# A graph network kernel: one-hots of the bucket count laid out by pairs of chunks, and last blocks zeroed in 19 calls of 128 lanes

## The chip, the cores and the metric

The kernel runs on one NeuronCore of a Trainium2 chip, the other seven idle. Its time is the device time of one execution in microseconds. A core has four compute engines, which are programmed separately and meet only at semaphores: PE (TensorE, matrix products into PSUM), DVE (VectorE), ACT (ScalarE) and POOL (GpSimd). SP (SyncE) only issues DMAs. POOL issues the indirect DMAs, whose row numbers come from a table in SBUF, one row per lane (partition).

## The reference

6250 nodes of 128 features, 100000 edges (source, target, a vector of 128, a type, a weight) sorted by target. Four graph layers follow each other, each with a sum over edges, dense products, and a normalisation:

```python
edge_index = jnp.stack([src, dst])
x = _layernorm(x + L0(x, edge_attr_128, ..., edge_index, batch0))    # edge vectors summed by source, MLP with batch norms
x = _layernorm(x + L1(x, edge_index, W, b))                          # mean of x[src] by target
x = _layernorm(x + L2(x, edge_index, edge_type_3, Wmsg, ...))        # mean of typed messages by target
x = _layernorm(x + L3(x, edge_index, edge_weight, W, ...))           # weighted, degree-normalised sum by target
```

Sums over edges are `segment_sum(rows[src], dst)`, or in L0 `segment_sum(edge_attr, src)`. The change touches none of the layers. It touches only how the kernel sorts its edges before the first one.

## The kernel before, in words

The nodes lie in 49 groups of 128 (`GROUPS`). Each edge belongs to one of 49 x 49 = 2401 buckets, by the group of its source and the group of its target. The kernel first writes all edges into a DRAM array `slots`, bucket after bucket, each bucket rounded up to blocks of four rows (`BLK`). With edges sorted so, a tile of 128 rows touches one group of nodes, and sums and gathers become products with one-hot matrices. This sorting comes in stages:

1. *Lists and keys* (to 11.5 us). SP loads sources, targets, types and weights as 128 x 784 tables. DVE shifts them to group numbers, `sg[:, 0, :]` (64 times the source's group) and `sg[:, 1, :]` (the target's), as bf16. POOL makes constants, `group_e` among them: `group_e[p, k, g, c]` is g, or 64 g for the source side, the same for all 14 values of c.
2. *Bucket count*. The 784 columns are handled in 56 batches of 14 (`HB`). `hot_pairs` (L1459) makes the one-hots of a batch for sources and targets in one DVE operation, `hot1[:, s]`, in two buffers s. `count_buckets` (L1085) makes seven matmuls of 98 x 98 (`PAIR`): each takes two chunks of 128 edges at once, chunks j and j + 7, and adds up the counts in PSUM. PE waits for `hot1_ready`, DVE for `hot1_used` of the batch before the last. After the last batch DVE copies the 98 x 98 table, of which only the parts where both chunks are the same are used.
3. *Tables* (85 to 92 us). DVE and PE turn the counts into first blocks (`first_b`), in a chain of small operations. `last_b` holds each bucket's last block, or a number out of range where the bucket is empty. It has 49 x 50 entries: one column is filled with a number out of range (L1502), so that 2450 = 98 x 25.
4. *Zeroing*. The last block of a bucket may be partly empty, so all its four rows (2176 B) are written with zeros first. SP sends `last_b` to DRAM (L483), waits, and reads it back as 98 x 25 (L485). POOL waits for both (`last_out`), makes 25 indirect DMAs of 98 lanes (L626), and waits until all have landed (L629).
5. *Scatter* (130 to 1500 us). 112 batches of seven chunks (`CB`), in a ring of four (`ARING`). For each: DVE makes one-hots (`show`), PE counts and looks up start rows (`count_batch`, `look_up`), ACT copies counts (L769) and edge payloads (L772), DVE works out row numbers (`place`, L1566), POOL scatters seven chunks (L642), SP refills edge rows and keys once the ring's buffer is free.

The order of SP's queue is written out by hand: lists, zero blocks of the spare region, edge rows, keys, node features, weights, then the index table (L482 to L485), then keys and edges of the ring. POOL's: constants, payload tables (L614 to L619, up to 29 us), waits (L621 to L624), zeroing, scatter. DVE starts the scatter batches without waiting for the zeroing; only POOL stands behind it. After 1500 us come the layers.

## Time and profile before

| | |
|---|---|
| median of 3 runs | 4760.21 us (4743.07 to 4760.88) |
| the profiled execution | 4730.64 us, span 4728.8 us |
| PE / DVE / ACT / POOL busy | 3121.7 / 2448.9 / 1101.7 / 1891.8 us |
| bucket count | 11.5 to 85 us |
| tables, index table out and back | 85 to 95 us |
| zeroing with its landing | 95 to 130.6 us |
| scatter | 130.6 to 1500 us |
| the four layers | 1500 to 4729 us |

The span is from the first to the last instruction on the core; all positions in time below count from its start. In the groups, the busy time of an engine is the time in which it executes, and "idle before" is how long it stood still ahead of these instructions, with what ended most of that. "SPq" or "POOLq" is the engine's queue, which issues DMAs. A DMA's duration on such a row is that of its issue, not of its transfer. Durations of a PE matmul overlap those of its neighbours.

### The profile page before, as it was taken

What the parts mean: (1) busy time and instruction counts of PE and PEld (TensorE: products, weight loads), DVE (VectorE), ACT (ScalarE), POOL (GpSimd) and SP (SyncE); (2) the same over time, 40 slices, a digit from 0 to 9 for tenths busy, and PEclk for the clock granted to TensorE, in tenths of its full rate; (3) what the DMA queues carried; (4) which work ended last, traced back from release to release, by engine and by line L of the source; (5) the groups of instructions that cost most, each with busy time, mean ns of one, the idle gap of its engine ahead of it and who ended that gap; (6) DMA issues with size and microseconds to landing.
All of it is one profiled execution on the core that took longest, in us unless ns stands there. A gap on an engine that the chain in (4) does not pass through costs nothing. (4 is left out here: it accounts for less than half of the span.)

```text
span 4728.8 us, 90919 instructions
## 1 busy us (share of the span) xinstructions
PE 3121.7 (66%) x22101; PEld 2714.0 (57%) x22102; DVE 2448.9 (52%) x6634; ACT 1101.7 (23%) x3584; POOL 1891.8 (40%) x1876
## 2 busy tenths in 40 slices
PE   7233333333334888677688788888888985777896
PEld 6121212122213775567678668888887875676785
DVE  6344445445445778422277743333335775222687
ACT  0010100000000114444322222111113206666302
POOL 3545456555553002466500035555554303556000
PEclk9999999999999999788899898888999997888998
DMA  6333333333333772566577344333336753666784
GB/s 193 107 95 101 95 107 107 111 108 105 107 112 105 237 235 81 172 220 222 176 237 231 121 139 127 122 120 121 127 104 196 230 176 122 210 217 208 221 265 141
DMA packets 499448, 736.58 MB, mean 156 GB/s; under 512 B 79317, under 2 KB 308702, under 8 KB 498382
## 3 DMA queue, kind: packets, MB, share of 16 engines
q1 hardware_dynamic: 404958, 498.38, 35.5%
q0 software_dynamic: 94448, 237.72, 13.7%
q8 instruction: 17, 0.28, 0.0%
q14 instruction: 25, 0.20, 0.0%
HBM read 486.89 MB, written 294.76 MB: 165 GB/s over the span
## 5 line engine op out<-in xcount | busy, mean ns | idle before, releaser
L688 POOL DMA_INDIRECT gbuf<-ring_raw,idx_blk x731 | 731.1, 1000 | 1167.2 <-DMA msg_rows<-big 425.1
L1206 PE MATMUL ps<-ring_raw,hot_raw 128*128 128x128 f32 (+2 forms) x8256 | 1027.4, 281 | 163.1 <-DVE hot_raw L1617 108.0
L1206 PEld LDWEIGHTS ps<-ring_raw,hot_raw 128*128 128x128 f32 x8256 | 969.9, 193 | 232.4 <-DVE hot_raw L1617 103.1
L642 POOL DMA_INDIRECT slots<-ring_raw,idx_edges x782 | 765.7, 979 | 607.2 <-DVE ring_raw L1566 362.4
L1232 PE MATMUL ps<-big,hot_raw 128*128 x5160 | 661.1, 293 | 124.1 <-ACT ring_raw L841 67.1
L1232 PEld LDWEIGHTS ps<-big,hot_raw 128*128 128x128 f32 x5160 | 643.8, 208 | 141.9 <-issue 140.9
L1130 PE MATMUL ps<-big 49*128 49x98 f16 x784 | 159.8, 256 | 564.8 <-ACT big L769 417.3
L1130 PEld LDWEIGHTS ps<-big 49*128 49x128 f16 x784 | 103.5, 136 | 589.8 <-issue 589.8
L1635 DVE TENSOR_TENSOR big<-big,ps 128x128 f32 (+2 forms) x1032 | 294.5, 285 | 255.1 <-PE ps L1206 216.1
L1617 DVE SCALAR_TENSOR_TENSOR hot_raw<-ring_raw,back,lane_ids 128x512 f32<-128x512 f32 x516 | 386.0, 748 | 64.0 <-DMA ring_raw<-gbuf 33.6
L1121 PE MATMUL ps<-big 128*49 128x343 bf16 (+6 forms) x784 | 264.2, 490 | 228.5 <-DVE big L1520 143.0
L1243 PE MATMUL ps<-big,hot_raw 128*128 x2064 | 315.2, 315 | 130.9 <-issue 76.5
L1243 PE MATMUL ps<-X,hot_raw 128*128 x2064 | 313.4, 313 | 121.2 <-issue 85.1
L841 ACT COPY ring_raw<-ps 128x512 f32<-128x512 f32 x473 | 277.0, 589 | 486.3 <-PE ps L1232 311.0
L1243 PEld LDWEIGHTS ps<-big,hot_raw 128*128 128x128 f32 x2064 | 291.5, 224 | 153.3 <-issue 150.8
L1243 PEld LDWEIGHTS ps<-X,hot_raw 128*128 128x128 f32 x2064 | 292.0, 225 | 142.9 <-issue 142.0
L1539 DVE TENSOR_TENSOR big<-big 49x49 f32<-49x49 f32 x112 | 22.9, 204 | 665.4 <-ACT big L769 517.4
L1663 DVE TENSOR_SCALAR hot_raw<-zr,row_t 128x512 f32<-128x512 bf16 x387 | 165.6, 487 | 322.0 <-PE ps L1232 158.6
L1121 PEld LDWEIGHTS ps<-big 128*49 128x49 bf16 x784 | 113.8, 159 | 372.8 <-issue 226.0
L1625 DVE TENSOR_TENSOR hot_raw<-dst_lane,lane_ids 128x1024 f32<-128x1024 f32 x258 | 318.2, 1234 | 14.2 <-issue 14.2
L769 ACT CAST big<-ps 49x343 f16<-49x343 f32 x112 | 49.3, 440 | 1142.3 <-remote 729.8
L1672 DVE TENSOR_SCALAR hot_raw<-zr,row_t 128x512 f32<-128x512 bf16 x258 | 126.2, 505 | 356.6 <-remote 147.8
(262 smaller groups left out, 3760.3 us busy)
## 6 DMA issues: line engine op xcount, KB each, us to landing
ring_raw<-gbuf SPq DMA_DIRECT2D x774, 268.0 KB
ring_raw<-slots SPq DMA_DIRECT2D x258, 272.0 KB
ring_raw<-in_edge_attr SPq DMA_DIRECT2D x111, 448.0 KB
zr<-lane_rows SPq DMA_DIRECT2D x387, 128.0 KB
zt<-lane_rows SPq DMA_DIRECT2D x344, 128.0 KB
pays_raw<-key_rows SPq DMA_DIRECT2D x112, 224.0 KB
big<-src_rows SPq DMA_DIRECT2D x112, 112.0 KB
slots<-ring_raw,idx_edges POOLq DMA_INDIRECT x782
```

What stands on the lines that cost most here:

```text
L642: pool.indirect_dma_start(edges, bass.IndirectOffsetOnAxis(idx_edges[0:n, u, j:j + 1], 0), edge_rows[0:n, u, j, :], None).then_inc(scatter ...
L688: pool.indirect_dma_start(gbuf, bass.IndirectOffsetOnAxis(idx_blk[:, r:r + 1], 0), node_rows[:, r, :], None, bounds_check=NBLK - 1, oob_is ...
L841: ins = act.copy(rows[:, :, 0:D], parts)
L1121: ins = pe.matmul(counts_of(s)[:, j * GROUPS:].rearrange("p (n g) -> p n g", g=GROUPS), hot2[:, s, 0, :, j], hot2[:, s, 1, :, j][:, None, ...
L1130: pe.matmul(to, hot, bases[:, s, 0, :], start=True, stop=False, skip_group_check=True)
L1206: ins = pe.matmul(bank(r % 3, width), hots[:, r, j * P:(j + 1) * P], rows[:, j, 0:width], start=j == 0, stop=j == BLK - 1)
L1232: ins = pe.matmul(bank(r)[:, j * P:(j + 1) * P], hots3[:, (odd + r) % 2, t, j * P:(j + 1) * P], msgs_flat[:, bass.ds(at[r] + t * D, D)], s ...
L1243: ins = pe.matmul(bank(r)[:, j * P:(j + 1) * P], hots[:, r, j * P:(j + 1) * P], nodes[:, bass.ds(at[r], D)], start=True, stop=True)
L1617: dve.scalar_tensor_tensor(out=hots[:, r, :].rearrange("p (k d) -> p k d", k=BLK), in0=key.broadcast_to([P, BLK, P]), scalar=back[:, k, ba ...
L1625: dve.tensor_tensor(hot_raw[:, 2 * h * BLK * P:(2 * h + 2) * BLK * P].rearrange("p (k d) -> p k d", d=P), lane.broadcast_to([P, 2 * BLK, P ...
L1635: dve.tensor_tensor(to, to, bank(r % 3, width), ALU.add).then_inc(added, 1)
L1663: ins = dve.tensor_scalar(hots3[:, (odd + r) % 2, t, :], lane_bc[r // LANE_SETS][:, r % LANE_SETS, :], row_t[:, t:t + 1], None, ALU.is_equal)
```

## The change

The one-hots get another layout. Before, `hot1[p, s, k, g, c]` had the 14 chunks innermost, and chunks j and j + 7 formed a pair: an operand of a matmul was every seventh element. Now `hot1[p, s, k, j, g, c]` has seven pairs j outside, and the two chunks of a pair (2j and 2j + 1) innermost, so an operand is 98 elements in a row. The comparison has four dimensions in this layout, so it is made in two operations of 686 elements, sources and targets apart. Which chunks form a pair doesn't change the counts.

The index table loses its extra column: 2401 entries are 18 x 128 + 97. It is read back by two DMAs, 128 x 18 and 97 x 1, and POOL makes 18 calls of 128 lanes and one of 97. POOL waits for `last_out` at 48, not 32.

```diff
--- before.py
+++ after.py
@@ -95,9 +95,9 @@
 ROW_G = D + 6
 AW = D + 5
 NOWHERE = 1.0e6
-LASTB = 25
-LASTP = 98
-assert LASTB * LASTP == GROUPS * (GROUPS + 1)
+LASTB = GROUPS * GROUPS // P
+LASTP = GROUPS * GROUPS - LASTB * P
+assert 0 < LASTP <= P
 
 HALF = STEP * P // 2
 EPS = 1e-5
@@ -172,7 +172,7 @@
         msg_rows = dram("msg_rows", [GROUPS * P * TYPES, D])
         key_rows = dram("key_rows", [COLS, P], I16)
         src_rows = dram("src_rows", [COLS, P], BF16)
-        last_blocks = dram("last_blocks", [GROUPS, GROUPS + 1], U32)
+        last_blocks = dram("last_blocks", [GROUPS, GROUPS], U32)
 
         X = sb("X", [P, GROUPS, D])
         big = sb("big", [P, 2 * GROUPS * D + GROUPS * AW])
@@ -206,7 +206,7 @@
             assert at + n <= GROUPS * AW
             return sums_flat[:, at:at + n], at + n
         hot1_f, at = work(0, 2 * GROUPS * HB)
-        hot1 = hot1_f.bitcast(BF16).rearrange("p (s k g c) -> p s k g c", s=2, k=2, g=GROUPS)
+        hot1 = hot1_f.bitcast(BF16).rearrange("p (s k j g c) -> p s k j g c", s=2, k=2, g=GROUPS, c=2)
         hot2_f, at = work(0, 2 * GROUPS * CB)
         hot2 = hot2_f.bitcast(BF16).rearrange("p (s k g c) -> p s k g c", s=2, k=2, g=GROUPS)
         src_hot_f, at = work(2 * GROUPS * HB, CB * P)
@@ -269,8 +269,8 @@
         first_b = sb("first_b", [GROUPS, 2, GROUPS])
         heads = sb("heads", [GROUPS, 12])
         heads_i = sb("heads_i", [GROUPS, 2], I32)
-        last_b = sb("last_b", [GROUPS, GROUPS + 1], U32)
-        zero_idx = sb("zero_idx", [LASTP, LASTB], U32)
+        last_b = sb("last_b", [GROUPS, GROUPS], U32)
+        zero_idx = sb("zero_idx", [P, LASTB + 1], U32)
         key_bc = pays_raw[:, COLS * PAY:COLS * PAY + ARING * CB * P // 2].bitcast(I16).rearrange(
             "p (s n) -> p s n", s=ARING)
         rank = sb("rank", [P, 2, CB])
@@ -482,8 +482,10 @@
             sp.wait_ge(last_ready, 1)
             sp.dma_start(last_blocks, last_b[:, :]).then_inc(last_out, 16)
             sp.wait_ge(last_out, 16)
-            sp.dma_start(zero_idx[:, :], last_blocks.rearrange("a b -> (a b)").rearrange(
-                "(p k) -> p k", k=LASTB)).then_inc(last_out, 16)
+            flat = last_blocks.rearrange("a b -> (a b)")
+            sp.dma_start(zero_idx[:, 0:LASTB], flat[0:P * LASTB].rearrange("(p k) -> p k", k=LASTB)).then_inc(last_out, 16)
+            sp.dma_start(zero_idx[0:LASTP, LASTB:LASTB + 1], flat[P * LASTB:GROUPS * GROUPS].rearrange(
+                "(p k) -> p k", k=1)).then_inc(last_out, 16)
 
             def next_keys(r, a):
                 if not first_of(r):
@@ -620,13 +622,14 @@
 
             pool.wait_ge(zero_done, 16 * 2 * ZSPAN // (P * BLK))
             pool.sem_inc(issued, 1)
-            pool.wait_ge(last_out, 32)
+            pool.wait_ge(last_out, 48)
             pool.sem_inc(issued, 1)
-            for k in range(LASTB):
+            for k in range(LASTB + 1):
+                n = P if k < LASTB else LASTP
                 pool.indirect_dma_start(
-                    slots, bass.IndirectOffsetOnAxis(zero_idx[:, k:k + 1], 0), zeros[0:LASTP, 0:BLK * ROW_A], None,
+                    slots, bass.IndirectOffsetOnAxis(zero_idx[0:n, k:k + 1], 0), zeros[0:n, 0:BLK * ROW_A], None,
                     bounds_check=NBLK - 1, oob_is_err=False).then_inc(last_zero, 16)
-            pool.wait_ge(last_zero, 16 * LASTB)
+            pool.wait_ge(last_zero, 16 * (LASTB + 1))
             pool.sem_inc(issued, 1)
 
             edges = slots.rearrange("b (k w) -> (b k) w", k=BLK)
@@ -1084,9 +1087,9 @@
 
             def count_buckets(b, s):
                 pe.wait_ge(hot1_ready, b + 1)
-                left, right = (hot1[:, s, k].rearrange("p g c -> p (g c)") for k in range(2))
+                left, right = (hot1[:, s, k].rearrange("p j g c -> p j (g c)") for k in range(2))
                 for j in range(HB // 2):
-                    ins = pe.matmul(ps[0:PAIR, 0, 0:PAIR], left[:, j::HB // 2], right[:, j::HB // 2],
+                    ins = pe.matmul(ps[0:PAIR, 0, 0:PAIR], left[:, j, :], right[:, j, :],
                                     start=first_of(b) and j == 0, stop=True, skip_group_check=True)
                 ins.then_inc(hot1_used, 1)
 
@@ -1457,8 +1460,11 @@
             dve.wait_ge(consts, 12)
 
             def hot_pairs(b, s):
-                dve.tensor_tensor(hot1[:, s], sg[:, :, None, bass.ds(b * HB, HB)].broadcast_to([P, 2, GROUPS, HB]),
-                                  group_e[:, :, :, :], ALU.is_equal).then_inc(hot1_ready, 1)
+                for k in range(2):
+                    ins = dve.tensor_tensor(hot1[:, s, k], sg[:, k, bass.ds(b * HB, HB)].rearrange(
+                        "p (j c) -> p j c", c=2)[:, :, None, :].broadcast_to([P, HB // 2, GROUPS, 2]),
+                                            group_e[:, k, None, :, 0:2].broadcast_to([P, HB // 2, GROUPS, 2]), ALU.is_equal)
+                ins.then_inc(hot1_ready, 1)
 
             for s in range(2):
                 hot_pairs(s, s)
@@ -1499,10 +1505,9 @@
             link(dve.tensor_scalar(next_rows, first_b[:, 0, :], float(BLK), -float(CENTRE), ALU.mult, ALU.add))
             link(dve.tensor_copy(bases[:, 0, 0, 0:GROUPS], next_rows))
             mark(dve.tensor_tensor(bases[:, 0, 1, 0:GROUPS], next_rows, bases[:, 0, 0, 0:GROUPS], ALU.subtract))
-            mark(dve.tensor_scalar(last_b[:, GROUPS:GROUPS + 1], heads[:, 0:1], 0.0, NOWHERE, ALU.mult, ALU.add))
             link(dve.tensor_scalar(blocks_f[:, 2, :], blocks_f[:, 0, :], 0.0, NOWHERE, ALU.is_equal, ALU.mult))
             link(dve.tensor_tensor(blocks_f[:, 2, :], blocks_f[:, 2, :], blocks_f[:, 0, :], ALU.add))
-            link(dve.scalar_tensor_tensor(out=last_b[:, 0:GROUPS], in0=first_b[:, 0, :], scalar=-1.0,
+            link(dve.scalar_tensor_tensor(out=last_b[:, :], in0=first_b[:, 0, :], scalar=-1.0,
                                           in1=blocks_f[:, 2, :], op0=ALU.add, op1=ALU.add))
             dve.sem_inc(last_ready, 1)
             dve.wait_ge(tables_turned, 4)
```

## Rows read from the trace of the kernel before

**Rows 1.** Table of stretches: length, each engine's busy us, granted clock, DMA share, GB/s.

```profile
95.00:128.00 33.00, 12.12 (x84) 7.42 (x82) 16.30 (x69) 1.72 (x6) 25.26 (x25) 1.00 0.62 193
130.00:1500.00 1370.00, 454.60 (x3007) 277.49 (x3008) 656.60 (x2615) 87.83 (x325) 765.05 (x782) 1.00 0.33 102
```

**Rows 2.** Waits, POOL, 130 to 1500 us: waiter, releaser, total us, times, longest.

```profile
POOL slots L642 <- DVE ring_raw L1566: 362.4, 50, 10.6
```

**Rows 3.** Timeline, 126 to 160 us: start, length, instruction, idle before and releaser.

```profile
130.57 0.99 POOL L642 DMA_INDIRECT slots<-ring_raw,idx_edges  x1 [2.82 <-issue]
...
147.01 0.96 POOL L642 DMA_INDIRECT slots<-ring_raw,idx_edges  x1 [0.30 <-issue]
...
149.86 0.44 ACT L769 CAST big<-ps 49x343 f16<-49x343 f32 x1 [40.38 <-remote]
...
154.54 1.01 POOL L642 DMA_INDIRECT slots<-ring_raw,idx_edges  x1 [6.57 <-DVE ring_raw L1566]
```

**Rows 4.** One-hots: 30 to 82 us (busy us, mean ns, idle); all (ns, first, last start).

```profile
L1460 DVE TENSOR_TENSOR big<-big,group_e 128x1372 bf16<-128x1372 bf16 x43 | 37.6, 874 | 16.3 <-PE ps L1089 16.3
...
L1460 DVE TENSOR_TENSOR big<-big,group_e x56: 859/874/1828, 11.5 to 82.6; 128x1372 bf16<-128x1372 bf16 x56
```

**Rows 5.** Timeline, 28 to 33 us: weight loads and one-hots of the bucket count.

```profile
30.21 2.29 PEld L1089 LDWEIGHTS ps<-big 128*98 128x98 bf16 x14 [0.20 <-DVE big L1460]
30.40 0.87 DVE L1460 TENSOR_TENSOR big<-big,group_e 128x1372 bf16<-128x1372 bf16 x1 [0.24 <-PE ps L1089]
...
32.89 0.87 DVE L1460 TENSOR_TENSOR big<-big,group_e 128x1372 bf16<-128x1372 bf16 x1 [0.24 <-PE ps L1089]
```

**Rows 6.** Timeline, 84 to 99 us: the index table out and back, first zeroing call.

```profile
90.44 0.14 DVE L1502 TENSOR_SCALAR last_b<-heads 49x1 uint32<-49x1 f32 x1
...
91.23 0.27 SPq L483 DMA_DIRECT2D last_blocks<-last_b  x1
...
92.54 0.32 SPq L485 DMA_DIRECT2D zero_idx<-last_blocks  x1
92.90 0.38 SPq L460 DMA_DIRECT2D pays_raw<-key_rows  x1
...
95.19 1.20 POOL L626 DMA_INDIRECT slots<-hot_raw,zero_idx  x1 [66.11 <-issue]
```

**Rows 7.** By line (L626, L688: ns min/median/max, first, last start; L439: landing us).

```profile
L626 POOL DMA_INDIRECT slots<-hot_raw,zero_idx x25: 956/961/1758, 95.2 to 126.8; - x25
...
L688 POOL DMA_INDIRECT gbuf<-ring_raw,idx_blk x731: 966/974/1406, 1921.5 to 4388.4; - x183
...
DMA to landing us min/median/max: 2.6/4.0/4.2
```

**Rows 8.** Timeline, 11.5 to 24 us: transposes and one-hots beside POOL.

```profile
11.56 1.54 PEld L1097 LDWEIGHTS ps<-ident_h,big 128*112 128x112 bf16 x14 [11.24 <-issue]
...
21.56 3.25 DVE L1460 TENSOR_TENSOR big<-big,group_e 128x1372 bf16<-128x1372 bf16 x2 [0.83 <-PE ps L1089]
```

**Rows 9.** DVE groups by form, 130 to 1500 us.

```profile
L1550 DVE TENSOR_TENSOR big<-ps,big 128x686 f32<-128x686 f32 x110 | 133.6, 1214 | 17.3 <-remote 17.3
L1555 DVE TENSOR_REDUCE found<-big 128x14 f32<-128x686 f32 x110 | 95.4, 868 | 3.8
L1520 DVE TENSOR_TENSOR big<-big,group_e 128x686 bf16<-128x686 bf16 x108 | 61.3, 568 | 11.0 <-issue 10.9
```

**Rows 10.** DVE groups by form, whole span: strided statistics reads.

```profile
L1703 DVE TENSOR_TENSOR mv<-stats 128x49 f32<-128x49 f32 x3 | 0.7, 246 | 0.1
L1703 DVE TENSOR_TENSOR mv<-stats 128x14 f32<-128x14 f32 x4 | 0.7, 184 | 0.1
```

**Rows 11.** Timeline, 90.9 to 136 us: two DVE operations in a row.

```profile
96.62 0.55 DVE L1520 TENSOR_TENSOR big<-big,group_e 128x686 bf16<-128x686 bf16 x1
...
97.09 0.44 DVE L1523 TENSOR_SCALAR big<-big,row 49x896 f16<-49x896 bf16 x1
```

## The prediction

> **What bounds the kernel now.** I read the table of time stretches first. From 130 to 1500 us the kernel scatters the edges: PE is 33%, DVE 48%, POOL 56% busy, DMA share 0.33; nothing is saturated [rows 1]. The list of POOL's waits says who holds whom there: 362 us of POOL's idle time ends with the DVE line that finishes a batch's positions [rows 2]. The timeline of that stage's start shows the reverse link: POOL's calls for the second batch end at 147.97 us (147.01 + 0.96), ScalarE's copy of the fourth batch's counts comes at 149.86, 40 us after its last instruction, and POOL's third batch follows at 154.54 [rows 3]. So the stage is a loop through POOL's own calls and their landing, and it is anchored at POOL's first scatter call. I expect a shift of that call (130.57 us) to reach the end of the kernel unchanged; what is left to ask is how far the change moves it.
>
> Two stretches lie ahead of that call. The first counts buckets in 56 batches: a DVE one-hot operation, then seven PE matmuls. The DVE operations start between 11.5 and 82.6 us; those after 30 us take 874 ns each, a row of 1372 bf16, and DVE is idle for 16.3 us waiting for PE [rows 4]. The timeline shows the rhythm: DVE starts at 30.40 and 32.89, two batches in 2.49 us, and PE's weight loads run 14 in 2.29 us without a gap [rows 5]. One batch costs 1.245 us, of which PE has 1.15. The second stretch zeroes the last blocks: the index table goes out (91.23), comes back (92.54), POOL makes 25 calls from 95.2 to 126.8, and the scatter starts 2.8 us after the last one ends [rows 3, 6, 7].
>
> **Fewer zeroing calls.** A POOL call takes 0.96 us with 0.30 idle ahead, 1.26 [rows 3]. 25 calls become 19 (18 of 128 lanes, one of 97), so 6 x 1.26 = 7.6 us go, if 128 lanes cost POOL what 98 do. They do in a near row: a 128-lane scatter of rows of almost the same length takes 974 ns in the median against 961 here [rows 7]; 19 x 0.013 = 0.2 us at most. The same 2401 rows of 2176 B (5.2 MB) now go out in 25 us, not 33, beside the other traffic: 193 GB/s at a DMA share of 0.62 [rows 1] becomes some 240 GB/s at 0.77. That is no saturation, so the wait for the last landing stays; for the lost slack I allow 1 us in the range.
>
> **A second read of the index table.** The tail of 97 indices is one more SP issue, and POOL waits for three landings in place of two. SP issues such transfers 0.36 us apart (92.54, 92.90) [rows 6], the lower bound. The old loads of 32 lanes x 4 B took up to 4.2 us to land [rows 7]; the table's way out was over after 1.3 us (91.23 to 92.54), so 4.2 - 1.3 + 0.4 = 3.3 us is the upper bound. I take 1.3 us, nearer the lower end, because the tail goes into an empty queue and is 97 elements long. Queued behind it on SP is the key load of the fourth batch; its keys are used long before POOL's third batch can go, so the delay is hidden. Behind POOL's wait stands only the zeroing.
>
> The Trainium skill ("DMA: Bandwidth & Descriptors", why a DMA increments its semaphore by 16) says that a transfer is spread over the largest number of DMA engines up to 16 that divides its slowest dimension; 97 is prime, so the tail would run on one. No row of before has such a transfer. By this rule the tail lies in the upper half of the bounds, at 2 us and not 1.3, and the sum is 0.7 us smaller.
>
> **The removed fill of the table's extra column** takes half of its 0.14 us from the DVE chain ahead of the table's way out, since DVE's instructions overlap by about that [rows 6]: 0.1 us.
>
> **The counting matmuls.** Both operands were read at a step of 14 bytes; now they are contiguous. A matmul with its load costs 164 ns now (2.29 us for 14). The nearest contiguous row is the 14 transposes of 112 x 128 bf16 at 11.56 us: 14 weight loads in 1.54 us, 110 ns each [rows 8]; seven cost 0.75 us at most. PE stops being the slower of the pair.
>
> **The one-hots.** One operation of 1372 elements becomes two of 686, whose table operand is now read two elements (4 bytes) at a time, 28 bytes apart; the key operand repeats one 4-byte word 49 times. What such a read costs is the step on which the sum turns.
> - 686 f32 contiguous take 868 ns [rows 9]: 1.04 ns each over a fixed 152 ns. The operation now, 874 = 152 + 686 x 1.05, moves two elements per tick.
> - Lower bound, short rows cost nothing: 152 + 343 x 1.04 = 509 ns.
> - Rows of seven bf16, the nearest by form: 568 ns for 686 elements [rows 9]. Pairs still run; the excess is 59 ns over 98 rows.
> - One source that hops at every element: 686 take 1214 ns [rows 9], 1.55 ns per tick.
> - Both sources hop by 24 bytes: 14 elements 184 ns, 49 elements 246 ns [rows 10], 1.77 ns per tick. Upper bound with pairs: 152 + 343 x 1.77 = 759 ns.
> I take 1.55, since one source hops and every tick does: 684 ns. Two operations in a row start 0.08 us closer than their length (0.55 long, the next 0.47 later, 96.62 and 97.09) [rows 11], so DVE's pace is 2 x 0.60 = 1.20 us per batch. The other limit, one buffer's cycle, is now 1.15 for PE + 0.87 for DVE + 0.47 of hand-over = 2.49; it becomes 0.75 + 0.60 + 0.68 + 0.40 = 2.43, or 1.21 per batch. From 30 to 82.6 us 42 x (1.245 - 1.21) = 1.5 us are gained. PE's gain is real, and DVE eats it.
>
> Before 30.4 us POOL works beside DVE, and six of the DVE operations last 1.2 to 1.8 us, as the two in 3.25 us at 21.56 [rows 8]; the excess is 3.5 us in all, in part hidden by DVE's waiting. With DVE the limit it is exposed: 13 x 1.21 + 3.5 = 19.2 us against 18.9 now (11.5 to 30.4), 0.3 lost. After the last batch PE has 0.4 us less to do. With the removed fill the counting stage gains 1.5 - 0.3 + 0.4 + 0.1 = 1.7 us.
>
> The Trainium skill ("Vector Engine (DVE) Microarchitecture Reference", 5.2, measured stream behaviour) speaks against this part: a port keeps its full rate only with runs of at least two adjacent 4-byte words, and one source that hops every word costs 1.73 ns per column. By that figure a batch costs DVE 1.33 us, the counting stage loses some 5 us, and the whole change gains 1. The rows show the effect at 1.55; none shows it with packed pairs.
>
> **Sum.** -7.6 + 1.3 - 1.7 = -8.0 us. The profiled execution took 4730.6 us (span 4728.8), so 4722.6 on its scale. It lies 29.6 us under the median of the runs shown, 4760.2, and 12.4 under the lowest; on the median's scale the forecast is 4752.
>
> **The rivals.**
> *B. Short rows are free.* The rows of seven speak for it (their 59 ns could be pairs that straddle rows, and with rows of two none does); the 1214 ns row speaks against. DVE 2 x 0.43; the cycle 0.75 + 0.43 + 0.51 + 0.40 = 2.09, 1.05 per batch: 42 x 0.195 = 8.2, before 30.4 us 3.5, with the rest 12.2. Sum -7.6 + 1.3 - 12.2 = -18.5: 4742. With PE at 80 ns per matmul it is 0.97 per batch and -23: 4737.
> *C. The repeated word counts as a hop too.* 759 - 83 = 676 ns, 1.35 per batch: +4.4, before 30.4 us +2.2, -0.5, and the zeroing's -6.3 is used up: 4760. For it speaks the 1.77; against it that only one source moves between words.
> *D. Rows of two lose the pair mode (slower than before).* The change then doesn't do what it says: DVE takes 686 ticks at 1.04 to 1.55 ns, 0.78 to 1.13 us per operation, 1.57 to 2.26 per batch. 42 batches lose 14 to 43 us, the 13 before 30.4 us 5 to 14; less 6.3 and 0.5, +12 to +50: 4772 to 4810. It is slower than before from 0.68 us per operation on. The rows of seven kept the mode, which speaks against.
> *E. The earlier start is not passed on:* the scatter loop meets its keys or edge rows later, and the time stays at 4760. Against it stands the link from landing to call above.
>
> **How the numbers follow.** Forecast 0.48, B 0.27, C 0.09, D 0.07, E 0.09. The runs before spread over 18 us, which adds to every case. 4728 to 4774 takes in B, C, E and the near end of D, and leaves out 0.1 on either side. About 0.5% (24 us) is what a measurement can tell from no change: faster than 4736 takes B's far end or a lucky spread, 0.12; slower than 4784 takes D, 0.06; the same 0.82.
>
> **What would show it.** One-hot operations of about 0.68 us, 1.21 us per batch and DVE hardly idle after 30 us; 0.51 and 1.05 mean B, 0.76 C, over 0.85 D. Weight loads 110 ns apart or less, and PE waiting for DVE. 19 zeroing calls 1.26 us apart, the first 4.0 us after the first read-back's issue, not 2.65. The first scatter call near 122.6 us, and the end of the scatter stage as much earlier. The prediction is wrong if that call moves by over 15 us or later, or if the stage behind it keeps its old end.

## Result: 0.3% slower, and the profile after

The changed kernel takes 4765.85 us in the median of 20 runs, the kernel before 4752.60 of 20 beside it: ratio 1.0032, 95% interval 1.0017 to 1.0047, so some 13 us slower where I forecast 8 us faster. The profiled execution of after took 4762.6 us with a span of 4760.7.

The timeline of POOL in the kernel after, from the payload operations to the first scatter calls (start, length, operation, idle before it):

```profile
10.31 1.93 POOL L616 MEMSET pays_raw<- 128x784 f32 x1
12.12 83.22 POOL L618 TENSOR_SCALAR pays_raw<-big 128x784 f32<-128x784 int32 x3
95.20 1.58 POOL L619 COPY pays_raw<-big 128x784 f32<-128x784 f32 x1
96.65 2.92 POOL L620 TENSOR_SCALAR pays_raw<-big 128x784 f32<-128x784 int32 x1
99.46 2.91 POOL L621 TENSOR_SCALAR pays_raw<-big 128x784 f32<-128x784 int32 x1
106.05 1.22 POOL L629 DMA_INDIRECT slots<-hot_raw,zero_idx  x1 [3.68 <-issue]
...
128.29 0.98 POOL L629 DMA_INDIRECT slots<-hot_raw,zero_idx  x1 [0.30 <-issue]
129.57 2.18 POOL L629 DMA_INDIRECT slots<-hot_raw,zero_idx  x1 [0.30 <-issue]
144.32 0.99 POOL L645 DMA_INDIRECT slots<-ring_raw,idx_edges  x1 [12.57 <-DVE ring_raw L1571]
```

The first scatter call, the anchor of the prediction, comes at 144.32 us; it was 130.57 [rows 3]: 13.75 us later. That is about what the median lost, though the interval alone would allow 8 to 22 us. The two profiled executions themselves lie 32 us apart (4762.6 and 4730.6): besides the 13.75 us, the scatter stage lasts 1387.0 us from its first call to its last in the one and 1369.2 in the other, though no line of that stage was changed.

Three things are to be seen in the rows. The first zeroing call comes 10.9 us later than 95.19 [rows 3, 6]. The 19 calls are as quick as forecast, one per 1.28 us, and end at 131.75, 25.7 us after the first one starts; before it was 32.56 (95.19 to 127.75). But behind the last one, which alone lasts 2.18 us, POOL stands idle for 12.57 us in place of 2.82 [rows 3]. The releaser named there, DVE's L1571, is a line of the stage's positions: it had written the first batch's at 114.94 us already, so the wait was for a DMA, the zeroing's own landing, as the experiments below show.

The ledger of the move is 10.86 + (25.70 - 32.56) + (12.57 - 2.82) = 10.86 - 6.86 + 9.75 = 13.75 us.

Where the first 10.86 come from, the count stage of after shows. DVE's group of instructions from 30 to 82 us (count, busy us, mean ns, idle before):

```profile
L1464 DVE TENSOR_TENSOR big<-big,group_e 128x686 bf16<-128x686 bf16 x77 | 52.7, 755 | 0.0
```

PE's group in the same stretch:

```profile
L1092 PE MATMUL ps<-big 128*98 128x98 bf16 x270 | 31.6, 288 | 20.8 <-DVE big L1464 20.8
```

The one-hot line over the whole kernel (lengths in ns min/median/max, first and last start):

```profile
L1464 DVE TENSOR_TENSOR big<-big,group_e x112: 746/756/1417, 11.9 to 89.0; 128x686 bf16<-128x686 bf16 x112
```

The table of time stretches (PE, PEld, DVE, ACT and POOL busy, granted clock, DMA share, GB/s):

```profile
30.00:50.00 20.00, 11.95 (x104) 9.53 (x102) 20.00 (x30) 0.00 (x0) 20.00 (x1) 1.00 0.93 252
50.00:70.00 20.00, 12.16 (x105) 9.86 (x105) 20.00 (x31) 0.00 (x0) 20.00 (x1) 1.00 0.69 176
```

A one-hot takes 756 ns, not 684. DVE has no idle time at all (16.3 us of it before [rows 4]), PE waits for it for 20.8 us, and POOL is "busy" from end to end with one single operation, its second payload comparison (same list of groups, 30 to 82 us):

```profile
L618 POOL TENSOR_SCALAR pays_raw<-big 128x784 f32<-128x784 int32 x1 | 77.1, 77106 | 0.0
```

The other comparisons of that size take about 3 us. A batch takes 1.37 us (weight loads at 28.32, 29.68 and 31.05 below), against 1.245 [rows 5]. PE did become quick: seven weight loads run in 0.66 us, 94 ns each, at the same granted clock of 1.00. The timeline of after, 28 to 33 us:

```profile
28.32 0.66 PEld L1092 LDWEIGHTS ps<-big 128*98 128x98 bf16 x7 [0.72 <-DVE big L1464]
29.68 0.66 PEld L1092 LDWEIGHTS ps<-big 128*98 128x98 bf16 x7 [0.70 <-DVE big L1464]
31.05 0.66 PEld L1092 LDWEIGHTS ps<-big 128*98 128x98 bf16 x7 [0.72 <-DVE big L1464]
```

So the copy of the 98 x 98 table comes at 90.67 us; in before it is at 85.00. That is 5.7 us. Then comes DVE's chain of small operations up to the index table (timeline of after):

```profile
90.67 0.26 DVE L1478 COPY tables<-ps 98x98 f32<-98x98 f32 x1 [0.91 <-PE ps L1092]
91.82 0.77 DVE L1484 CAST small_i<-tables 49x49 int32<-49x49 f32 x1
92.63 0.67 DVE L1485 TENSOR_SCALAR small_i<-small_i 49x49 int32<-49x49 int32 x1
...
94.44 2.36 DVE L1495 COPY heads<-tables 49x2 f32<-49x2 f32 x1
...
100.94 0.20 DVE L1510 SCALAR_TENSOR_TENSOR last_b<-first_b,tables 49x49 uint32<-49x49 f32 x1
```

The same chain in the kernel before (timeline, 84.5 to 96 us):

```profile
85.00 0.26 DVE L1472 COPY tables<-ps 98x98 f32<-98x98 f32 x1 [1.48 <-PE ps L1089]
...
87.70 0.16 DVE L1489 COPY heads<-tables 49x2 f32<-49x2 f32 x1
...
90.94 0.20 DVE L1505 SCALAR_TENSOR_TENSOR last_b<-first_b,tables 49x49 uint32<-49x49 f32 x1
```

10.3 us in after, 5.9 in before. A copy of 49 x 2 numbers lasts 2.36 us, and 0.16 us in before. POOL's payload operations, which before had ended by 29.1 us, run just here: the one that was held for 77 us ends at about 92.4, soon after DVE's first idle time (0.91 us ahead of the copy at 90.67), and the rest follows until 102.37. That makes 4.3 us. The last 0.9 is the second read-back: 4.91 us from the end of L1510 to the first zeroing call in after, 4.05 in before.

### The profile page after: what moved, and what is told of

Its sections match the earlier page's. It is cut to its first block, busy times and chain, and to the rows that moved or that the text cites. A ratio compares the mean times of both kernels' runs of the same rounds, so it can differ in the third digit from the quotient of the medians.

```text
span 4760.7 us, 91017 instructions
## 1 busy us (share of the span) xinstructions
PE 3107.1 (65%) x22101; PEld 2692.3 (57%) x22102; DVE 2478.0 (52%) x6689; ACT 1101.7 (23%) x3584; POOL 1963.0 (41%) x1870
## 4 chain that ended last, share of the span: by engine, by line
PE 31%; another core or an unknown queue 22%; issue 18%; DVE 11%; DMA 6%; ACT 5%; DVEq 3%; SPq 2%; POOL 1%; ACTq 1%; POOLq 0%
PE ps L1235 11%; PE ps L1209 10%; PE ps L1246 3%; DMA gbuf<-ring_raw,idx_blk 2%; PE ps L1124 2%; DMA ring_raw<-slots 2%; ACT ring_raw L841 2%; DMA ring_raw<-gbuf 2%; DVE hot_raw L1630 2%; DVEq L428 1%; DVE hot_raw L1622 1%; POOL gbuf L691 1%; PE ps L1283 1%; DVE big L1464 1%
## 5 line engine op out<-in xcount | busy, mean ns | idle before, releaser
L1668 DVE TENSOR_SCALAR hot_raw<-zr,row_t 128x512 f32<-128x512 bf16 x387 | 164.9, 488 | 321.1 <-PE ps L1235 147.4
L841 ACT ACTIVATE ring_raw<-ps,pays_raw 128x128 f32<-128x128 f32 x1032 | 280.3, 412 | 27.0 <-remote 12.7
```

Of the source, the lines that this page charges most:

```text
L841: ins = act.activation(rows[:, j, 0:D], parts[:, j, :], ACT.Copy, scale=pays_raw[:, bass.ds(at * (BLK * PAY) + (j * PAY + P_W), 1)])
```

## The experiments

The kernels are called by their first letters, a to k, where that is plain.

All ratios are against runs of the kernel before on the same chip at the same time. Beside the kernels a to d the kernel before took 4160 us in the median, beside e to g 4165, and beside h to k 4747. Most of that difference is in the scatter stage (998 to 999 us from its first call to its last there, 1360 to 1387 in the other traces), the rest behind it. One chip showed both, so it is no matter of the chip; its cause wasn't looked for. POOL's scatter calls show what it means for this document. The group of these calls in the kernel before and in `c_after_pad` (below), whole span:

```profile
L642 POOL DMA_INDIRECT slots<-ring_raw,idx_edges x782 | 765.7, 979 | 607.2 <-DVE ring_raw L1566 362.4 <-issue 244.8
L646 POOL DMA_INDIRECT slots<-ring_raw,idx_edges x782 | 761.1, 973 | 241.2 <-issue 238.1 <-DVE ring_raw L1573 3.0
```

In the second, as in all seven traces a to g, POOL goes from call to call with 0.30 us between (241 to 254 us idle for 782 calls), so the stage is as long as its calls, wherever it starts. In the other six traces POOL stands idle for 598 to 635 us, 359 to 410 of them for DVE's positions, and there the stage's length varies. The stages up to the first scatter call agree: the copy of the 98 x 98 table comes at 84.97 to 85.40 us in the five traces with the old one-hots and the early payload operations (before, b, d, f, h). By these stages I read the experiments.

**The two halves apart, and the last call with 128 lanes.** My theory was the ledger above: the late landing comes from the last call's 97 lanes, and the first call's delay from the one-hots.

`a_hots_only`: the new layout (`hot1`, `hot_pairs`, `count_buckets`), zeroing as before.

```
-                dve.tensor_tensor(hot1[:, s], sg[:, :, None, bass.ds(b * HB, HB)].broadcast_to([P, 2, GROUPS, HB]),
-                                  group_e[:, :, :, :], ALU.is_equal).then_inc(hot1_ready, 1)
+                for k in range(2):
+                    ins = dve.tensor_tensor(hot1[:, s, k], sg[:, k, bass.ds(b * HB, HB)].rearrange(
+                        "p (j c) -> p j c", c=2)[:, :, None, :].broadcast_to([P, HB // 2, GROUPS, 2]),
+                                            group_e[:, k, None, :, 0:2].broadcast_to([P, HB // 2, GROUPS, 2]), ALU.is_equal)
+                ins.then_inc(hot1_ready, 1)
```

> The kernel before with the new one-hot layout alone; zeroing stays at 25 calls of 98 lanes. Theory (ledger of the two traces: the one-hots cost 5.7 us themselves, and the payload operations of GpSimd that they push behind the count stretch VectorE's table chain by another 4.3): first zeroing call at 105.2 us, first scatter call at 140.6 (130.6 + 10.0), no late landing (under 3 us from the last zeroing call's end to the first scatter call), time +10 us against before (ratio 1.0021). Rival 1 (late landing comes from the shifted start, which meets other traffic, and not from the last call's 97 lanes): the first scatter call comes over 8 us after the last zeroing call here too. Rival 2 (start is not passed on, the scatter stage's rhythm made the 13 us): the time stays within 3 us of before although the first scatter call is 10 us later.

Measured: first zeroing call 105.29, first scatter call 140.66 us, 2.86 us idle ahead of it; 1.0026 (1.0016 to 1.0037), +11 us.

`b_zero_only`: the zeroing of after, one-hots as before.

```
-LASTB = 25
-LASTP = 98
+LASTB = GROUPS * GROUPS // P
+LASTP = GROUPS * GROUPS - LASTB * P
```

> The kernel before with the zeroing in 19 calls alone (18 of 128 lanes, the last of 97); one-hots as before. Theory (the last call's 97 rows all go out by one DMA engine): first zeroing call 96.1 us (+0.9 for the second read-back), last call's end 121.8, then some 12.5 us until the first scatter call at 134.4, +3.8 us against before; time +4 us (1.0008). Rival 1: the landing wait stays under 3 us, first scatter call at 124.6, time -6 us. Rival 2: the time doesn't follow the first scatter call.

Measured: 1.0015 (1.0004 to 1.0025), +6 us. The timeline of POOL at the end of the zeroing:

```profile
119.53 0.97 POOL L629 DMA_INDIRECT slots<-hot_raw,zero_idx  x1 [0.30 <-issue]
120.81 2.18 POOL L629 DMA_INDIRECT slots<-hot_raw,zero_idx  x1 [0.30 <-issue]
135.99 0.98 POOL L645 DMA_INDIRECT slots<-ring_raw,idx_edges  x1 [13.00 <-issue]
```

The late landing stands here with the old one-hots. The half that I had priced at -6.3 us makes the kernel slower by itself.

`c_after_pad` and `d_zero_pad`: the last call has 128 lanes, in the kernel after and in `b_zero_only`.

```
+            dve.memset(zero_idx[:, LASTB:LASTB + 1], 1000000).then_inc(padded, 1)
...
-                n = P if k < LASTB else LASTP
...
-                    slots, bass.IndirectOffsetOnAxis(zero_idx[0:n, k:k + 1], 0), zeros[0:n, 0:BLK * ROW_A], None,
+                    slots, bass.IndirectOffsetOnAxis(zero_idx[:, k:k + 1], 0), zeros[:, 0:BLK * ROW_A], None,
```

> The kernel after, but the last zeroing call has 128 lanes, too: the 31 lanes beyond the table hold 1000000 and are skipped by the bounds check. The read-back of 97 indices is unchanged. Theory (one DMA engine for 97 lanes): wait from the last call's end to the first scatter call 2.8 us in place of 12.6, first scatter call at 134.6, time 9.8 us under after's, +4 against before (1.0008). Rival 1 (fuller calls queue up in the DMA engines, or the traffic beside it is late): the wait stays over 8 us, time as after's (1.003).

> The kernel before with the zeroing in 19 calls of 128 lanes (31 of the last padded and skipped), one-hots as before. Theory: both costs are gone, first zeroing call 96.1, first scatter call at 124.6 (130.6 - 6.0), time -6 us against before (0.9987). Rival 1: late landing stays, +4 us. Rival 2 (start not passed on): 0.

Measured: c first scatter call 134.87 us, 1.0020 (1.0010 to 1.0030), +8 us; d 124.44 us, 0.9994 (0.9982 to 1.0006), -2.5 us. The same stretch of `d_zero_pad`:

```profile
119.15 0.97 POOL L630 DMA_INDIRECT slots<-hot_raw,zero_idx  x1 [0.30 <-issue]
120.43 0.97 POOL L630 DMA_INDIRECT slots<-hot_raw,zero_idx  x1 [0.30 <-issue]
124.44 0.96 POOL L646 DMA_INDIRECT slots<-ring_raw,idx_edges  x1 [3.03 <-DVE ring_raw L1570]
```

31 lanes more, and the last call takes 0.97 us and not 2.18, the wait 3.03 and not 13.00. Traffic, fuller calls and the shifted start are the same as in b, so that rival falls. In all four the scatter stage lasts 998 to 999 us from the first call to the last (c: 134.9 to 1133.3; d: 124.4 to 1122.0), so the start is passed on to that stage's end in full. In the total it can't be shown so finely: c lies 4 us above and d 3.5 above what the start says, which is the edge of c's interval and within d's.

Why 97 lanes land late, the transfers of after show, taken as a table of time stretches (DMA share and GB/s are the last two columns):

```profile
100.00:128.00 28.00, 10.07 (x61) 5.85 (x61) 14.77 (x69) 1.14 (x4) 19.43 (x18) 1.00 0.60 210
134.00:142.60 8.60, 5.44 (x47) 3.78 (x47) 7.63 (x29) 0.57 (x2) 0.00 (x0) 1.00 0.07 23
142.60:145.00 2.40, 0.57 (x2) 0.24 (x3) 2.30 (x9) 0.00 (x0) 0.68 (x1) 1.00 0.00 0
```

The packets of 134 to 142.6 us in the view of the DMA:

```profile
DMA packets 45, 0.20 MB, mean 23 GB/s; under 512 B 1, under 2 KB 1, under 8 KB 44
```

From 134 to 142.6 us a share of 0.07, about one DMA engine of sixteen (0.0625), moves 0.20 MB, of which 0.18 are 44 packets of POOL's queue; the 97 rows of 2176 B are 0.21 MB. The Trainium skill ("DMA: Bandwidth & Descriptors", why a DMA increments its semaphore by 16) has the rule that I applied to the read-back of the tail alone; this scatter's share of one engine agrees with it: 97 is prime, 98 is 14 x 7, 128 is 16 x 8.

One thing more stands in the counts of the DMA's packets, and it belongs to the cost. POOL's queue (packets, MB, share of 16 engines) over the whole zeroing, in the kernel before (25 calls of 98 lanes, 95 to 129.5 us) and in `f_all97` below (25 calls of 97 lanes, 96 to 204 us); then all packets of after from 130.5 to 134 us, just ahead of the 44 above:

```profile
q0 software_dynamic: 2000, 5.23, 48.2%
...
q0 software_dynamic: 20000, 5.37, 33.0%
...
DMA packets 776, 0.05 MB, mean 14 GB/s; under 512 B 766, under 2 KB 766, under 8 KB 776
```

A call of 98 lanes leaves as 80 packets, one of 97 as 800, for nearly the same bytes. In the same way the 19 calls of after make 2240 (18 x 80 + 800) and the 19 of `d_zero_pad` 1520 (19 x 80), both with 5.23 MB. Of the 800 some 750 are under 512 B, and they go first. My reading is an estimate from these counts: 80 is 16 x 5 and 800 is 16 x 50, as if each of the sixteen engines got as many packets as the busiest one needs: 97 rows on one engine are 49 packets of up to two rows and one more, 7 or 8 rows (98 lanes on 14 engines, 128 on 16) are four and one more. What the small packets are, and whether they are why POOL itself takes longer over such a call, no run shows.

**The same cost put on every call.** `f_all97`: 25 calls of 97 lanes.

```
+LASTL = 97
+LASTB = GROUPS * GROUPS // LASTL
...
-                n = P if k < LASTB else LASTP
+                n = LASTL
```

> The kernel before with the zeroing in 25 calls of 97 lanes (the last with 24 padded lanes that are skipped), one-hots as before: the suspected cost of the last call is put on every call. Theory (a call of 97 lanes goes out by one DMA engine, 97 rows at some 87 ns of that engine each = 8.4 us, and takes GpSimd 2.18 + 0.30 us): 25 calls take 62 us in place of 32; if all calls fall on the same engine the landing ends 25 x 8.4 = 210 us after the first call, first scatter call near 308 us and the time +178 us (1.04); if they fall on different engines, first scatter call near 96 + 62 + 8 = 167 us, +36 us (1.009). Rival (the late landing in after is a matter of the whole load, not of the number 97): calls 1.26 us apart, first scatter call within 4 us of before's.

Measured: 1.0172 (1.0152 to 1.0192), +72 us; first scatter call 203.66 us. Neither of my two cases, but the rival is far off. POOL's timeline:

```profile
116.23 2.14 POOL L632 DMA_INDIRECT slots<-hot_raw,zero_idx  x1 [0.30 <-issue]
118.68 2.15 POOL L632 DMA_INDIRECT slots<-hot_raw,zero_idx  x1 [0.31 <-issue]
137.85 2.15 POOL L632 DMA_INDIRECT slots<-hot_raw,zero_idx  x1 [17.03 <-issue]
...
185.39 2.14 POOL L632 DMA_INDIRECT slots<-hot_raw,zero_idx  x1 [0.30 <-issue]
203.66 0.99 POOL L648 DMA_INDIRECT slots<-ring_raw,idx_edges  x1 [16.13 <-issue]
```

Every call takes 2.15 us. After ten, and again after twenty, POOL stands still for 17.0 and 13.5 us; what it waits for the trace doesn't name. The calls do not all fall on one engine: at 8.6 us of one engine each they would take 215 us, and they take 107. Nor do the engines share them well. From 120 to 130 us the DMA share is 0.75, but at 75 GB/s, with 1625 of 1777 packets under 512 B from 121 us on; from 130 to 150 us it is 0.18 at 33 GB/s and from 190 to 203 0.16 at 36. The kernel before moves its 193 GB/s at 0.62 [rows 1].

**What a one-hot's 756 ns are made of.** `e_forms`: before the count, with POOL's payload operations over, six comparisons of each of six forms, all of 686 bf16.

```
+            dve.wait_ge(pays_ready, 7)
...
+            for k in range(6):
+                dve.tensor_tensor(turn(), word, hop, ALU.is_equal).then_inc(form_done, 1)
+            for k in range(6):
+                dve.tensor_tensor(turn(), word, pairs, ALU.is_equal).then_inc(form_done, 1)
...
```

> The kernel after with the padded last call; ahead of the count VectorE waits until GpSimd's seven payload operations are over, and then makes six additional comparisons of each of six forms, all 686 bf16 from two sources, whose results are overwritten: (1) repeated word and table at a step of 28 bytes, as in the new one-hots, (2) repeated word and a table of adjacent pairs, (3) adjacent keys and the table at a step of 28 bytes, (4) both adjacent, (5) rows of 14 as in the old layout, (6) rows of 98. The output stays right. It asks what the 756 ns of a new one-hot are made of. Theory H (every hop of a source costs, pairs run: 152 + 343 x 1.77): form 1 759 ns, form 2 and 3 684 or less, forms 4 and 6 about 510. Rival M (the pair mode is gone as soon as a row has two elements, whichever source it is): forms 1, 2 and 3 about 756 and form 6 under 560. Rival G (GpSimd's pending operation slows VectorE): form 1 well under 756 here, since GpSimd is idle. Also: with GpSimd's work done before, the table chain between the copy of the 98 x 98 counts and the table's way out takes 6.2 us as in before, not 10.5, if GpSimd's late operations stretched it; if it stays at 10.5 it is something else of the new layout.

The timeline of DVE; the six lines are the forms 1 to 6, each row six operations:

```profile
27.55 4.17 DVE L1479 TENSOR_TENSOR big<-big,group_e 128x686 bf16<-128x686 bf16 x6 [16.14 <-POOL pays_raw L624]
31.64 2.63 DVE L1481 TENSOR_TENSOR big<-big,group_e 128x686 bf16<-128x686 bf16 x6
34.19 4.17 DVE L1483 TENSOR_TENSOR big<-big,group_e 128x686 bf16<-128x686 bf16 x6
38.28 2.64 DVE L1485 TENSOR_TENSOR big<-big,group_e 128x686 bf16<-128x686 bf16 x6
40.83 2.64 DVE L1487 TENSOR_TENSOR big<-big,group_e 128x686 bf16<-128x686 bf16 x6
43.38 2.64 DVE L1489 TENSOR_TENSOR big<-big,group_e 128x686 bf16<-128x686 bf16 x6
```

There are two prices only. Whatever reads the table at a step of 28 bytes (1 and 3) takes 4.17 us for six, 758 and 768 ns each; everything else takes 504 to 515 ns: the repeated word (2) costs nothing over adjacent keys (4), and a row of two nothing over rows of 14 or 98 (5, 6). Theory H is half right: a hop costs that much, but a word that repeats is no hop. M and G fall: form 2 has the same rows of two at the full pair rate (152 + 343 x 1.04 = 509), and form 1 takes its 758 ns with POOL idle. The chain behind the count, 124.05 to 129.94, takes 5.9 us, so its 10.3 in after came from POOL's late operations. The one execution took 4193.83 us, 29 more than before, with its first scatter call 33 us later.

**The layout without the hop.** `g_pair_table`: as `c_after_pad`, with the table copied to adjacent pairs.

```
+        group_p = sb("group_p", [P, 2, GROUPS, 2], BF16)
...
+                pool.tensor_copy(group_p[:, k, :, :], group_f[:, k, :, 0:2]).then_inc(pairs_made, 1)
...
-                                            group_e[:, k, None, :, 0:2].broadcast_to([P, HB // 2, GROUPS, 2]), ALU.is_equal)
+                                            group_p[:, k, None, :, :].broadcast_to([P, HB // 2, GROUPS, 2]), ALU.is_equal)
```

> The kernel after with the padded last call, and the one-hots' group table copied beforehand to adjacent pairs (392 bytes a lane for both sides), so that this source moves on without a hop; the key word still repeats 49 times. Theory H (a hop of each source costs): 684 ns or less per operation, spacing 0.60, 1.21 us per batch as before's 1.245, VectorE idle a little, GpSimd gets its turns, time within 3 us of the kernel before with 19 padded calls (0.9994 of before). Rival M (rows of two lose the pair mode): 756 ns, 1.37 us per batch, GpSimd held off, time as the kernel after with the padded call (1.002).

Measured: 0.9954 (0.9939 to 0.9969), -19 us, far better than either case. I had put half the hop's price on a hop that does not exist. First zeroing call 83.59 us, first scatter call 111.95. Its stretch from 30 to 60 us in the table of time stretches:

```profile
30.00:60.00 30.00, 24.79 (x213) 19.91 (x213) 27.20 (x62) 0.00 (x0) 0.46 (x1) 0.50 0.95 267
```

The same stretch of `i_pairs_only` (below):

```profile
30.00:60.00 30.00, 24.78 (x213) 19.83 (x212) 27.25 (x61) 0.00 (x0) 0.53 (x1) 1.00 0.97 271
```

30.4 batches in 30 us, 0.99 us each in place of 1.37, and POOL is done by 31 us. In g's profile the granted clock of PE is 0.50 (1.2 GHz) from 19 to some 1100 us, in i's 1.00 (2.4 GHz), and both make the same 213 matmuls. PE's instructions are no longer at the lower level: a matmul takes 288 ns in the mean of these 30 us in both, a weight load 194. Ahead of the fall PE was busy for 0.53 of the 2 us from 15 to 17 in g (0.83 in i, which kept its level) and for 1.03 of the next two (1.33 in i). The mean clock of whole executions says that it is no matter of g alone: 0.78 to 0.82 in two of the six runs of g, three of the eight of i and three of the 13 of j (below), 0.93 to 0.96 in every run of every other kernel. Seven of these eight took no longer than the others of their kernel. What made it fall isn't shown.

**Two halves again, one read-back, gaps for POOL.** `h_before` is the kernel before again, for its trace beside i, j and k.

> The kernel before, unchanged, for its trace on a chip like those of the other experiments, where it takes 4160 us and not 4750. Expected if the later stages alone differ between the chips: first zeroing call 95.2 us and first scatter call 130.6 as in the first trace, scatter stage 999 us from its first to its last call as in the other experiments (1369 in the first trace). If the earlier stages differ too, the ledgers of the experiments must be taken against this trace and not against the first.

Measured: first zeroing call 95.56, first scatter call 130.84 us, as in the first trace; scatter stage 1380.9 us and 4748.75 in all, like the kernel before in the first comparison. The 999 us that I expected for the stage did not come. The stages ahead of it are the same, so the earlier ledgers stand.

`i_pairs_only`: layout and pair table as in g, zeroing in 25 calls of 98 lanes.

> The kernel before with the new one-hot layout and the table of adjacent pairs; zeroing stays at 25 calls of 98 lanes. It is the first half of the change without the table's hop. Theory (only the table's hop made the layout dear, and its gain comes through): first zeroing call at 82.8 us, first scatter call at 118.1 us, time -12.5 us against before (0.9970). Rival (the two halves interact, the gain of g_pair_table needs the 19 calls): 0.9985 or more.

Measured: first zeroing call 83.25, first scatter call 118.24 us as expected; time 0.9940 (0.9918 to 0.9962), -28 us. The sign is the theory's, the size is beyond it: in the profiles the scatter stage was 11 us shorter than `h_before`'s, and where it is that long its length varies (1360 to 1387 us over six traces) for no reason that I found. The 12.6 us of the first scatter call lie outside the interval (18 to 39 us), and the part beyond them is not explained.

`j_one_read`: g with a single transfer for the table's way back.

```
-            sp.dma_start(zero_idx[:, 0:LASTB], flat[0:P * LASTB].rearrange("(p k) -> p k", k=LASTB)).then_inc(last_out, 16)
-            sp.dma_start(zero_idx[0:LASTP, LASTB:LASTB + 1], flat[P * LASTB:GROUPS * GROUPS].rearrange(
-                "(p k) -> p k", k=1)).then_inc(last_out, 16)
+            sp.dma_start(zero_idx[:, :], last_blocks.rearrange("(p k) -> p k", k=LASTB + 1)).then_inc(last_out, 16)
```

> g_pair_table with one read-back in place of two: the 31 indices beyond the table are written to DRAM early, and the 128 x 19 table comes back in one transfer. Theory: the second read-back costs 0.9 us, so the first zeroing call comes at 82.8 us and the first scatter call at 111.1, time -20 us against before (0.995). Rival (the transfer itself is longer, rows of 19 not 18 words, 128 lanes in both): no difference to g_pair_table, first zeroing call at 83.7. It also shows whether TensorE's granted clock falls to 0.50 in the count stage again, as in g_pair_table's profile, or stays at 1.00; at 1.00 the stage should be some us shorter (PE 0.66 us per batch, VectorE 0.86).

Measured: from the end of the table's last operation (78.91 + 0.20) to the first zeroing call (83.18) 4.07 us, g 4.92: the second read costs 0.85. The call itself comes only 0.4 earlier than g's, since this execution's count started 0.4 later. 0.9951 (0.9930 to 0.9972), -23 us. PE was granted 1.00 here, and the stage was not shorter: in that I was wrong.

`k_pauses`: `c_after_pad`, but in 16 batches VectorE waits for the batch just before.

```
+            for i in range(1, 9):
+                for s in range(2):
+                    dve.wait_ge(hot1_used, i * 2 + s)
+                    hot_pairs(i * 2 + s, s)
```

> The kernel after with the padded last call; in the batches 2 to 17 of the count VectorE waits until TensorE has used the batch just before, not the one before that, so it is idle for some 0.7 us after each pair of one-hots. Theory S (VectorE's unbroken two-source operations keep GpSimd's second payload operation from finishing; gaps let it through): GpSimd's seven payload operations are over by 40 us in place of 102, the table chain from the copy of the counts to the table's way out takes 6.2 us in place of 10.5, and the first zeroing call comes 16 x 0.8 = 13 us later for the waits and 4.3 earlier for the chain, at 114.7 us. Rival (GpSimd waits for something else than gaps on VectorE, or the chain is slow by itself): payload operations end after 95 us again, first zeroing call at 119.

The timeline of POOL:

```profile
12.10 8.88 POOL L620 TENSOR_SCALAR pays_raw<-big 128x784 f32<-128x784 int32 x3
20.85 1.58 POOL L621 COPY pays_raw<-big 128x784 f32<-128x784 f32 x1
22.31 3.39 POOL L622 TENSOR_SCALAR pays_raw<-big 128x784 f32<-128x784 int32 x1
25.57 3.13 POOL L623 TENSOR_SCALAR pays_raw<-big 128x784 f32<-128x784 int32 x1
119.44 1.23 POOL L630 DMA_INDIRECT slots<-hot_raw,zero_idx  x1 [90.74 <-issue]
```

The three comparisons that lasted 83.22 us in after last 8.88, and all is done at 28.7 us. The first zeroing call is at 119.44, as the rival had it, but by another sum: the waits cost 18.0 us (table copy at 108.40, c 90.36) and not 13, and the chain took 5.9 us (108.40 to 114.30). Gaps on DVE are what POOL needs. So the 83 us are theory S, and it is a matter of gaps, not of the operations' length, which is the same 763 ns as in c. The total, 4739.14 us in one execution, can't be used: it lies 8 us under the median of before beside it although the first scatter call comes 16.6 us later, and its scatter stage is the shortest of the six, 1360.2 us.

Milestones in us, from the timelines:

| | copy of the 98 x 98 table | first zeroing call | first scatter call | ratio to before |
|---|---|---|---|---|
| before | 85.00 | 95.19 | 130.57 | 1 |
| after | 90.67 | 106.05 | 144.32 | 1.0032 |
| a_hots_only | 90.48 | 105.29 | 140.66 | 1.0026 |
| b_zero_only | 85.40 | 96.39 | 135.99 | 1.0015 |
| c_after_pad | 90.36 | 105.75 | 134.87 | 1.0020 |
| d_zero_pad | 84.97 | 96.06 | 124.44 | 0.9994 |
| e_forms | 124.05 | 135.07 | 163.43 | 1.007 (one run) |
| f_all97 | 84.98 | 96.26 | 203.66 | 1.0172 |
| g_pair_table | 72.58 | 83.59 | 111.95 | 0.9954 |
| h_before | 85.26 | 95.56 | 130.84 | 1.000 (one run) |
| i_pairs_only | 72.65 | 83.25 | 118.24 | 0.9940 |
| j_one_read | 73.01 | 83.18 | 112.09 | 0.9951 |
| k_pauses | 108.40 | 119.44 | 147.13 | 0.998 (one run) |

g, i and j beat both kernels; among them the intervals overlap. By the first scatter call, g and j are the best.

## Why the prediction was wrong, step by step

- **Fewer zeroing calls, the step that failed most.** -7.6 us was nearly right for POOL: -6.86 measured, with 1.28 us per call of 128 lanes and 2.18 for the last. "The wait for the last landing stays" was the error: it grew by 9.75 us. I had named the rule of the DMA engines for the tail's read-back, and in the same change the last scatter call has the same 97 lanes, with rows of 2176 B each. `b`, `c`, `d` and `f` show it.
- **The second read-back.** 1.3 us forecast, 0.86 measured, and 0.85 in `j` against g.
- **The one-hots, the second step that failed.** The counting stage was to gain 1.7 us and lost 5.7. I took 1.55 ns per tick from a row of f32 that hops; the measured (756 - 152) / 343 is 1.76, the upper bound that I had worked out, and 1.37 us per batch is rival C's number (1.35). C's reason is false, though: the repeated word costs nothing, the table's hop costs all of it. The other figure in the prediction, 1.33 us per batch and 5 us lost in the count stage (the Trainium skill, "Vector Engine (DVE) Microarchitecture Reference", 5.2, 1.73 ns per column), was the good one: this trace has 1.37 and 5.7. I took a row of another data type over a figure for a very near pattern.
- **PE's contiguous operands.** 0.75 us for seven at most, 0.66 measured. That gain was eaten by DVE as forecast, and more than eaten.
- **POOL beside DVE, missing from the sum.** I priced it at 0.3 us, as POOL stretching DVE's operations before 30 us. I did not ask the reverse, what a VectorE without any idle time does to POOL: its comparison lasted 77 us, and its remaining work fell beside the table chain, 4.3 us. The Trainium skill ("SBUF — State Buffer", who interferes with whom) says that the port pair that the two engines share is an exclusive lock. That the loser waits fully agrees with the 83.22 us against 8.88 in `k`; why POOL doesn't get its turn between two back-to-back operations no run here shows.
- **The link from the first scatter call to the end.** Right where it could be tested: the stage behind it keeps its length in the traces of the seven kernels a to g (998 to 999 us), and the sign and rough size of their times follow. But there POOL's calls alone set the stage's length. The loop with waits that the prediction describes is that of the other six traces, and in them the length varies from 1360 to 1387 us. For these the link rests on the medians: 13 us against 13.75 in the main comparison, 21 against 18.8 for j, and 26 against 12.6 for i, so it is not shown to a few us.
- **The range** did hold 4765.85, on the slower side of its centre; its chance for a loss was on rival D alone, with a mechanism that did not occur. That the time lies in it is luck: the call on which the forecast hangs moved the other way.

With the terms as measured the forecast would have been +5.7 + 4.3 + 0.9 - 6.9 + 9.8 = +13.8 us.

## What to carry to other kernels

Count for every DMA that a change touches how many DMA engines its lanes divide into: a last call of 97 lanes put the first scatter call 9.5 us (after against c) and 11.6 us (b against d) later than one padded to 128 with indices that are skipped, more than six calls fewer had saved. When an operation is laid out anew, look at each source for itself: one that steps on at every tick doubles the price of a tick's excess, and a small copy of the table in the order in which it is read turned a loss of 5.7 us in the stage into a gain of 12.4. And when a change takes away an engine's idle time, ask who lived on it.

## What the runs showed of the hardware

- VectorE, two bf16 sources, 686 elements, measured with POOL idle: 504 to 515 ns with a repeated 4-byte word, rows of 2, 14 or 98, or adjacent; 758 to 769 ns as soon as one source steps 28 bytes between words.
- PE's matmul with its weight load, 98 x 98 bf16 at the granted clock 1.00: 164 ns with both operands at a step of 14 bytes [rows 5], 94 ns with adjacent ones.
- An indirect scatter of 2176-byte rows: 97 lanes hold POOL for 2.18 us and 128 lanes for 0.97; 97 lanes make 800 DMA packets, 98 or 128 lanes 80. The rows of the 97 lanes go out at the share of one DMA engine, 44 of their packets in 8.6 us. Between the tenth such call in a row and the eleventh POOL stood for 17 us.
- A POOL comparison of 128 x 784 takes 3 us beside a VectorE with gaps and 77 us beside one without.
- A granted clock of 0.50 on TensorE in place of 1.00 left the mean length of its 98 x 98 matmuls (288 ns) and weight loads (194 ns) as it was, in the count stage of g against i.
